# A two-layer graph network: POOL no longer drained at block ends, last iteration of the second loop written out, last two node units on places of their own

## The chip, the cores and the metric

One core of one Trainium2 chip runs the whole program. The metric is the device time of one execution in microseconds; the median of several runs counts. Engines are named as in the profile: PE (matmul), PEld (its weight load), DVE (vector), ACT (scalar), POOL (GpSimd) and SP (the sync engine, which here only issues DMAs). A trailing q (POOLq, SPq, PEldq) is the engine's sequencer.

## The reference, cut to what matters

6250 nodes of 128 features, 106250 edges sorted by receiver. Two layers, each with a residual and a layer norm around it:

```python
x = layernorm(x + L0(x, edge_attr_3, edge_weight, src, dst))        # loop 1
# L1, loop 2:
msg_in = concat(x[src], x[dst]); per type t: h = relu(msg_in @ W1[t] + b1[t]); m = h @ W2[t] + b2[t]
msgs = m * sigmoid(msg_in @ attn_w[t] + attn_b[t]) where edge_type == t
agg  = zeros.at[dst].add(msgs)
r = sigmoid(gi_r + gh_r); z = sigmoid(gi_z + gh_z); n = tanh(gi_n + r * gh_n)   # gi = agg@w_ih+b_ih, gh = x@w_hh+b_hh
y = layernorm((1-z)*n + z*x + x)*gamma + beta                        # what L1 returns
out = layernorm(x + y)
```

The inner layer norm takes (1-z)n + zx + x; the outer one is taken over the sum with x once more. So each node goes through: sums, gates, candidate, blend, transposition to rows, a first norm, gamma, x, beta, a second norm, store.

## The kernel before, in words

**Blocks.** The program is a row of blocks: `prepare` (tables, indices and the first gathers; its block is line 335), `edges0` (loop 1, line 717), `leftover0` (line 1172, work that is skipped when nothing is left), `edges1` (loop 2, line 1531), `leftover1` (line 1172 again). Within a block each engine runs its own list and they meet by semaphores; at a block's end every engine executes a DRAIN and then all meet at a barrier before the next block begins.

**Loops.** Both loops run over 104 steps of 1024 edges (8 tiles of 128), in 26 iterations of 4 steps (SLOTS), one for each of four gather buffers. `gather_loop` (line 605 in `gather_step`) makes POOL issue 8 indirect DMAs for each step; before it issues them it waits that the buffer was used (`used`). `prepare` already issues the gathers of steps 0 to 2 of loop 1, loop 1's block those of step 3 on. Loop 1 needs them in `messages` (line 659), loop 2 in `edge_rows` (line 1906).

**A step j of loop 2.** PE multiplies, for step j + 1, windows of the receivers' table (`receivers`, line 1754). DVE adds the gathered rows (`hid`, line 1906), builds the receivers' one-hot for step j + 2 (`rows_hot`, line 1865), adds step j - 1's sums to the accumulator (`adds`, lines 1887 and 1890, each 4 pairs), builds the one-hot of step j + 1 (`one_hot`, line 1873) and the scores (line 1922). ACT takes score and relu (lines 1651 and 1655) and issues the window loads of step j + 2 (`load_windows`, line 1535) and a key row of step j + 4 (`load_row`). PE then forms the step's sums (lines 1818 and 1824), for which `adds` waits.

**Node units.** In the same loop, 3 iterations behind, units of 256 nodes whose sums are complete go through the update, spread over the steps: PE `node_sums` (lines 1764, 1765), ACT `copy_sums` (1661), PE `node_gates` (1773, 1774), ACT `gates` (1666), PE `node_candidates` (1778, 1779), DVE `candidate` (1951, 1954), ACT tanh (1671), DVE `blend` (1959 to 1965), PE `node_rows` (1785), DVE `new_rows` (1970 and `moments`, 1928 to 1936), `residual` (1944 to 1984 and `moments`), `result` (1944), SP `store` (1611). SP loads x (`load_x_t` 1603, `load_x_row` 1607). All units share one set of buffers (`unit_area`) and two PSUM banks (`ps_v`).

**The tail.** Units 0 to 21 are finished within the loop; unit 22 is blended in the last step. After the loop come the last `adds(103)`, the rows of unit 22 and, one behind the other in the shared buffers, units 23 (256 nodes) and 24 (the last 128). There POOL takes the inverse square roots (`pow`, line 1642), between gathers none. The order on PE and DVE is written out:

```python
node_rows(g - 1, UN); node_sums(g, n, STEPS); node_gates(g, n); node_candidates(g, n)        # PE
node_sums(g2, n2, STEPS); node_rows(g, n); node_gates(g2, n2); node_candidates(g2, n2); node_rows(g2, n2)
adds(STEPS - 1, 1); new_rows(g - 1); candidate(g); residual(g - 1); blend(g); result(g - 1)   # DVE
new_rows(g); candidate(g2); residual(g); blend(g2); result(g); new_rows(g2); residual(g2); result(g2)
```

SP handles each unit in the order load x_t, store of the unit before, load x_row. `new_rows` waits until the store of the unit before has landed, since it writes the same `mid`. The last iteration does some work for steps 104 and 105, which do not exist: window loads in steps 102 and 103, a receivers' one-hot in both, `receivers` and `one_hot` in step 103.

## Time and profile before

| | us |
|---|---|
| median of 3 runs (2250.91 to 2253.52) | 2253.49 |
| profiled execution, its own time | 2254.85 |
| its span, first to last instruction | 2253.1 |
| busy: PE, DVE, ACT, POOL | 1810, 1477, 1347, 1609 |
| loop 1's gathers, first to last issue | 54.8 to 1112.1 |
| loop 2's gathers, first to last issue | 1149.3 to 2199.7 |

Times in the rows are microseconds from the span's start, unless marked ns. "Idle before <- X" is how long the engine stood still before an instruction and what ended it; "issue" means nothing that the profile shows. Busy shares are averages over stages with different limits, so the stages are read one by one: two long loops, the seams between blocks, and a tail of about 50 us after the last gather.

### The profile page before, as it was taken

The numbers are of one execution on the slowest core, as the hardware profiler recorded it, in microseconds if no ns is written. First come the engines' busy times: TensorE is split into PE (matmuls) and PEld (weight loads), VectorE is DVE, ScalarE is ACT, GpSimd is POOL, SyncE is SP. The second block draws the span as 40 slices with busy tenths as digits, with TensorE's granted clock in tenths as the row PEclk, the third lists the DMA queues.
The fourth block names the chain that finished last, engine by engine and source line by source line (L and its number), as shares of the span: only waits on it lengthen the run. The fifth ranks groups of instructions, "written<-read, shape, count | busy, mean of one in ns | idle before, by whom it ended". The sixth has DMA issues, their size and how long they took to land. (4 is left out here: it accounts for less than half of the span.)

```text
span 2253.1 us, 43663 instructions
## 1 busy us (share of the span) xinstructions
PE 1810.1 (80%) x10012; PEld 1436.0 (64%) x10012; DVE 1476.7 (66%) x3701; ACT 1347.0 (60%) x4416; POOL 1608.6 (71%) x1699
## 2 busy tenths in 40 slices
PE   7598999999999999999867876766667666676664
PEld 4276666666666766666646766666656666666663
DVE  4566555555655656556546777777777777777775
ACT  2587877777777777777634544544545545454451
POOL 2777777777777777777546777777777777777771
PEclk7599999999999999999979988887887888888886
DMA  6522323323233232333257855445454544544541
GB/s 205 153 54 56 79 74 82 80 72 87 75 82 80 73 85 75 81 80 82 67 168 210 225 118 123 109 118 115 111 122 108 120 115 110 123 109 117 117 110 32
DMA packets 222343, 236.65 MB, mean 105 GB/s; under 512 B 73015, under 2 KB 163295, under 8 KB 222157
## 3 DMA queue, kind: packets, MB, share of 16 engines
q0 software_dynamic: 53808, 112.80, 21.9%
q10 hardware_dynamic: 90012, 58.96, 10.4%
q1 hardware_dynamic: 78481, 64.43, 9.4%
q8 instruction: 14, 0.23, 0.0%
q14 instruction: 28, 0.23, 0.0%
HBM read 191.66 MB, written 44.35 MB: 105 GB/s over the span
## 5 line engine op out<-in xcount | busy, mean ns | idle before, releaser
L605 POOL DMA_INDIRECT gx<-node_d,idx x832 | 798.9, 960 | 265.8 <-issue 259.6
L605 POOL DMA_INDIRECT gp<-p_tab_d,idx x832 | 792.1, 952 | 261.5 <-issue 251.5
L677 ACT ACTIVATE msg<-ws,y 128x32 f32<-128x32 f32 x2496 | 552.8, 316 | 64.5 <-DVE ws L656 64.1
L908 PEld LDWEIGHTS ps_a<-hot,msg 128*128 128x128 f32 x3328 | 408.5, 197 | 194.4 <-issue 113.2
L1754 PE MATMUL ps_e<-win,hot_x 128*128 128x129 f32 x1680 | 300.2, 351 | 272.4 <-DVE hid L1906 249.5
L908 PE MATMUL ps_a<-hot,msg 128*128 128x128 f32 x3328 | 431.8, 285 | 61.5 <-DVE msg L665 40.2
L1754 PEld LDWEIGHTS ps_e<-win,hot_x 128*128 128x128 f32 x1680 | 275.8, 256 | 295.2 <-DVE hid L1906 266.0
L659 DVE TENSOR_TENSOR vy<-gx,y 128x768 f32<-128x768 f32 x104 | 99.6, 958 | 334.1 <-DMA gx<-node_d,idx 334.0
L1655 ACT ACTIVATE hid<-hid,score 128x128 f32<-128x128 f32 x832 | 278.7, 395 | 10.1
L1906 DVE TENSOR_TENSOR hid<-ps_e,gp 128x387 f32<-128x387 f32 (+1 forms) x312 | 142.0, 510 | 147.2 <-DMA gp<-p_tab_d,idx 140.0
L638 PE MATMUL ps_w<-w,h 128*128 128x256 f32 x832 | 221.5, 412 | 0.0
L1818 PEld LDWEIGHTS ps_g<-hot,hid 128*128 128x128 f32 x1664 | 212.9, 200 | 7.7 <-issue 1.1
L1818 PE MATMUL ps_g<-hot,hid 128*128 128x128 f32 x1664 | 212.6, 283 | 0.9 <-ACT hid L1655 0.7
L1651 ACT ACTIVATE score<-hid 128x3 f32<-128x3 f32 (+1 forms) x312 | 61.3, 196 | 245.2 <-DVE hid L1906 240.5
L638 PEld LDWEIGHTS ps_w<-w,h 128*128 128x128 f32 x832 | 158.2, 200 | 67.2 <-issue 48.0
L186 ACT ACTIVATE h<-ps_h,b 128x512 f32<-128x512 f32 x208 | 142.1, 683 | 95.4 <-PE ps_h L191 83.2
L1865 DVE TENSOR_TENSOR hot_x<-key_row,ps_s 128x1024 f32<-128x1024 bf16 x106 | 128.4, 1212 | 32.7 <-PE ps_s L1824 28.2
L1887 DVE TENSOR_TENSOR acc<-acc,ps_g 128x128 f32 x416 | 119.5, 287 | 13.5 <-issue 0.9
L1873 DVE TENSOR_TENSOR hot<-ps_s,key 128x1024 f32<-128x1024 f32 x105 | 127.6, 1215 | 0.0
L1005 DVE TENSOR_TENSOR hot<-ps_a,dloc 128x1024 f32<-128x1024 f32 x104 | 126.6, 1217 | 0.0
L904 PE MATMUL ps_h<-emb,w 16*128 16x512 f32 x202 | 113.2, 640 | 0.0
L191 PE MATMUL ps_h<-h,w 128*128 128x512 f32 x208 | 109.6, 609 | 3.7 <-ACT h L186 3.7
(221 smaller groups left out, 2213.7 us busy)
## 6 DMA issues: line engine op xcount, KB each, us to landing
win<-q_tab_d ACTq DMA_DIRECT2D x416, 64.5 KB
key_row<-key_row_d ACTq DMA_DIRECT2D x102, 256.0 KB, 3.6
gx<-node_d,idx POOLq DMA_INDIRECT x832
gp<-p_tab_d,idx POOLq DMA_INDIRECT x832
p_tab_d<-acc SPq DMA_DIRECT2D x23, 516.0 KB
q_tab_d<-unit_area SPq DMA_DIRECT2D x36, 258.0 KB, 3.3
q_tab_d<-acc SPq DMA_DIRECT2D x5, 774.0 KB, 5.5
emb<-emb_d SPq DMA_DIRECT2D x102, 32.0 KB
```

The costliest lines, as they stand in the source:

```text
L186: e.activation(mlp[f"h{layer}"][:], mlp["ps_h"][:], ACT.Silu, bias=w[f"b{layer - 1}"][:]).then_inc(ok, 1)
L605: e.indirect_dma_start(out=buf[:, h, t, :], out_offset=None, in_=table, in_offset=bass.IndirectOffsetOnAxis(ap=idx[:, h, t:t + 1], axis=0) ...
L638: last = e.matmul(ps_w[:, 2 * t:2 * t + 2, :], h2[:, t * P:(t + 1) * P], w["w2"][:], start=False, stop=t % 2 == 1)
L677: last = e.activation(self.cols[1][:, tile, c, :], self.ws[:, tile, :], ACT.Copy, scale=y[:, c:c + 1])
L908: last = e.matmul(ps_a[:, h, b, :], msgs[h].tile(t, b), hot[:, h, t, :], start=t == 0, stop=t == TPS - 1)
L1005: e.tensor_tensor(hot[:, h], spread(ps_a[:, h, IOTA, :], 1, TPS), spread(w["dloc"][:, bass.ds(j * TPS, TPS)], 2, P), ALU.is_equal)
L1655: last = e.activation(hid[:, h, t, 0:H], hid[:, h, t, 0:H], ACT.Relu, scale=score[:, h, t:t + 1])
L1754: last = e.matmul(ps_e[:, q, at:at + PW], hot_x[:, h, t, :], win[:, h, t // 2, :], start=True, stop=True)
L1818: e.matmul(ps_g[:, h, t // 2, :], hid[:, h, t, 0:H], hot[:, h, t, :], start=t % 2 == 0, stop=t % 2 == 1)
L1865: e.tensor_tensor(hot_x[:, h].rearrange("p t n -> p (t n)"), key_row[:, h, :], part.to_broadcast([P, TPS * P]), ALU.is_equal).then_inc(hx_ ...
L1873: e.tensor_tensor(hot[:, h], spread(iota[:, 0:P], 1, TPS), spread(k["key"][:, tiles], 2, P), ALU.is_equal).then_inc(hot_ok, 1)
L1906: e.tensor_tensor(hid[:, h, mine, :], ps_e[:, q, 0:n * PW].rearrange("p (t n) -> p t n", t=n), gp[:, u, mine, :], ALU.add).then_inc(pre_ok, 1)
```

## The change

Three things are done. (1) All blocks are made with `no_gpsimd_drain=True`, so POOL no longer executes a DRAIN at their ends; it still takes part in the barrier. The semaphores that only carry waits (`gate`, `gate_x`, `gate_v`) become one. (2) The last iteration of loop 2 leaves its loop on PE and DVE (on ACT it was already written out), and the work for steps 104 and 105 is gone from it. In step 103 DVE does `adds(102)` ahead of `edge_rows` and `blend(22)` ahead of the scores; PE does `node_sums` of unit 23 in the place of `receivers`. For that, the lower bound of the window of step 103 (and of none before it) rises from node 5888 to 6144; its edges begin at node 6203. (3) Units 23 and 24 get buffers and banks of their own: unit 23 keeps the usual places but for x_t, x_row and mid, which lie in gather buffer 1; unit 24 has all in gather buffer 0 and the banks of `ps_e`, with counters of its own; unit 22's rows go to a third bank. Their loads wait for steps 100 and 101 to have used the buffers, and stand ahead of the stores. The written-out orders of SP, POOL, ACT, PE and DVE behind the loop are interleaved.

```diff
+BOUND = (NT - 1) * P
+            gate=m.sem("gate"),
...
-        with nc.Block() as block:
+        with nc.Block(no_gpsimd_drain=True) as block:
...
-                own.then(e.scalar_tensor_tensor(startf[:], past, float(LAST), startf[:], ALU.min, ALU.max))
+                own.then(e.scalar_tensor_tensor(startf[:], past, float(BOUND), startf[:], ALU.min, ALU.max))
...
+        usual = dict(places(unit_area, UN), sums=ps_u[:, 0], gates=ps_u[:, 1], rows=ps_u[:, 1], at=0, own_f=own_f, own_n=own_n,
+                     var_ok=var_ok, root_ok=root_ok)
+        spare = [gp[:, u].rearrange("p t f -> p (t f)") for u in range(2)]
+        before_rest = dict(usual, rows=ps_e[:, 2])
+        first_rest = dict(usual, at=2, **{name: spare[1][:, c * UN:(c + 1) * UN] for c, name in enumerate(("x_t",))},
+                          **{name: spare[1][:, c * UN:(c + 1) * UN].rearrange("p (b f) -> p b f", f=H)
+                             for c, name in ((1, "x_row"), (2, "mid"))})
+        last_rest = dict(places(spare[0], P), sums=ps_e[:, 0], gates=ps_e[:, 1], rows=ps_e[:, 1], at=4, own_f=end_f, own_n=end_n,
+                         var_ok=end_var, root_ok=end_root)
...
+                for (g, n), z, u in zip(REST, (first_rest, last_rest), (1, 0)):
+                    e.wait_ge(used, SLOTS + STEPS - SLOTS + u + 1)
+                    e.wait_ge(xt_ld, 16 * g)
+                    load_x_t(g, n, z)
+                    e.wait_ge(xr_ld, 16 * g)
+                    load_x_row(g, n, z)
+                store(UNITS - 1, UN, usual)
+                for (g, n), z in zip(REST, (first_rest, last_rest)):
+                    store(g, n, z)
...
-                    e.wait_ge(win_in[h], 16 * PPS * (STEPS // 2 + 1))
-                    e.wait_ge(row_in[h], 16 * (STEPS // 2 + 1))
+                    e.wait_ge(win_in[h], 16 * PPS * (STEPS // 2))
+                    e.wait_ge(row_in[h], 16 * (STEPS // 2))
...
-                for g in range(UNITS - 1, UNITS + 2):
-                    for c in range(2):
-                        e.wait_ge(var_ok, g * 2 + (c + 1))
-                        e.tensor_tensor(rstd[:], rstd[:], minus_half[:], ALU.pow).then_inc(root_ok, 1)
+                def root(g, n, c, z):
+                    mine = rstd[:, z["at"]:z["at"] + n // P]
+                    e.wait_ge(z["var_ok"], own_count(g, z) * 2 + (c + 1))
+                    e.tensor_tensor(mine, mine, minus_half[:, 0:n // P], ALU.pow).then_inc(z["root_ok"], 1)
+
+                (g, n), (g2, n2) = REST
+                for c in range(2):
+                    root(g - 1, UN, c, before_rest)
+                for c in range(2):
+                    root(g, n, c, first_rest)
+                    root(g2, n2, c, last_rest)
...
-                        e.wait_ge(e_mm, i * (NQ * SLOTS) + (NQ * u + NQ))
+                        if not last or u < SLOTS - 2:
+                            e.wait_ge(e_mm, i * (NQ * SLOTS) + (NQ * u + NQ))
-                        load_windows(e, regs, j + 2, h)
+                        if not last or u < SLOTS - 2:
+                            load_windows(e, regs, j + 2, h)
...
-                        if not last or u + SLOTS < SLOTS + 2:
+                        if not last:
...
-                for g, n in REST:
+                (g, n), (g2, n2) = REST
+                copy_sums(g, n, first_rest)
+                gates(g, n, first_rest)
+                copy_sums(g2, n2, last_rest)
+                candidate(g, n, first_rest)
+                gates(g2, n2, last_rest)
+                candidate(g2, n2, last_rest)
...
-                    e.wait_ge(cand_ok, g + 1)
+                    if z is not last_rest:
+                        e.wait_ge(cand_ok, g + 1)
...
-                    e.wait_ge(mid_ok, g + 1)
+                    if z is usual:
+                        e.wait_ge(mid_ok, g + 1)
                     for c in range(2):
...
-                def steps(i, unit, before, table=False):
+                def steps(i, unit, before, table=False, final=False):
                     for u in range(SLOTS):
                         h, j = u % 2, i * SLOTS + u
-                        e.wait_ge(hx_ok, j + 2)
-                        e.wait_ge(win_in[1 - h], i * (16 * PPS * SLOTS // 2) + 16 * PPS * (u // 2 + 1 + h))
-                        for q in range(NQ):
-                            e.wait_ge(pre_ok, i * (NQ * SLOTS) + (NQ * u + q + 1))
-                            receivers(1 - h, q)
+                        if not final or u < SLOTS - 1:
+                            e.wait_ge(hx_ok, j + 2)
+                            e.wait_ge(win_in[1 - h], i * (16 * PPS * SLOTS // 2) + 16 * PPS * (u // 2 + 1 + h))
+                            for q in range(NQ):
+                                e.wait_ge(pre_ok, i * (NQ * SLOTS) + (NQ * u + q + 1))
+                                receivers(1 - h, q)
+                        else:
+                            node_sums(*REST[0], STEPS - 1, first_rest)
...
-                with e.Fori(LAG + 1, LOOPS) as i:
+                with e.Fori(LAG + 1, LOOPS - 1) as i:
                     steps(i, True, True)
+                steps(LOOPS - 1, True, True, final=True)
...
-                node_rows(g - 1, UN)
-                node_sums(g, n, STEPS)
-                node_gates(g, n)
-                node_candidates(g, n)
-                node_sums(g2, n2, STEPS)
-                node_rows(g, n)
-                node_gates(g2, n2)
-                node_candidates(g2, n2)
-                node_rows(g2, n2)
+                node_rows(g - 1, UN, before_rest)
+                node_gates(g, n, first_rest)
+                node_candidates(g, n, first_rest)
+                node_sums(g2, n2, STEPS, last_rest)
+                node_gates(g2, n2, last_rest)
+                node_candidates(g2, n2, last_rest)
+                node_rows(g, n, first_rest)
+                node_rows(g2, n2, last_rest)
...
-                    if before:
-                        e.wait_ge(sum_mm, j)
-                    rows_hot(h, i * (16 * SLOTS // 2) + 16 * (u // 2 + 2))
+                    if not final or u < SLOTS - 2:
+                        if before:
+                            e.wait_ge(sum_mm, j)
...
                         e.wait_ge(zero_ok, 5)
-                    if before:
+                    if final and u == SLOTS - 1:
+                        blend(i - LAG, UN)
+                    elif before:
                         adds(j - 1, 1 - h)
-                    one_hot(bass.ds(j * TPS + TPS, TPS), 1 - h)
+                    if not final or u < SLOTS - 1:
+                        one_hot(bass.ds(j * TPS + TPS, TPS), 1 - h)
...
+                def new_rows(g, n, z=usual):
-                    e.wait_ge(y_st, g * 16 + 16)
-                    e.tensor_copy(mid[:, 0:n // P, :], ps_u[:, 1, 0:n].rearrange("p (b f) -> p b f", f=H))\
+                    if z is usual or z is before_rest:
+                        e.wait_ge(y_st, g * 16 + 16)
...
+                def steps(i, first, unit, before, last=False):
                     for u in range(SLOTS):
-                        edge_rows(i, u, not first or u > 0, first and u == 1)
+                        if last and u == SLOTS - 1:
+                            adds(STEPS - 2, 0)
+                        edge_rows(i, u, not first or u > 0, first and u == 1, last)
...
-                        if unit and u == 3:
+                        if unit and u == 3 and not last:
...
-                with e.Fori(LAG + 1, LOOPS) as i:
+                with e.Fori(LAG + 1, LOOPS - 1) as i:
                     steps(i, False, True, True)
+                steps(LOOPS - 1, False, True, True, last=True)
                 adds(STEPS - 1, 1)
...
-                new_rows(g - 1, UN)
-                candidate(g, n)
-                residual(g - 1, UN, True)
-                blend(g, n)
-                result(g - 1, UN, True)
-                new_rows(g, n)
-                candidate(g2, n2)
-                residual(g, n, True)
-                blend(g2, n2)
-                result(g, n, True)
-                new_rows(g2, n2)
-                residual(g2, n2, True)
-                result(g2, n2, True)
+                new_rows(g - 1, UN, before_rest)
+                candidate(g, n, first_rest)
+                residual(g - 1, UN, before_rest, True)
+                candidate(g2, n2, last_rest)
+                blend(g, n, first_rest)
+                result(g - 1, UN, before_rest, True)
+                blend(g2, n2, last_rest)
+                new_rows(g, n, first_rest)
+                new_rows(g2, n2, last_rest)
+                residual(g, n, first_rest, True)
+                residual(g2, n2, last_rest, True)
+                result(g, n, first_rest, True)
+                result(g2, n2, last_rest, True)
```

## Rows read from the trace of the kernel before

**Rows 1.** Waits of DVE over the whole span: engine, line <- awaited: us, times, longest
```profile
DVE vy L659 <- DMA gx<-node_d,idx: 334.0, 94, 5.6
DVE hid L1906 <- DMA gp<-p_tab_d,idx: 140.0, 90, 3.1
```

**Rows 2.** Line L605, POOL's gathers: ns min/median/max, and what its idle time ended on
```profile
L605 POOL DMA_INDIRECT gx<-node_d,idx x832: 942/947/2987, 54.8 to 1112.1; - x167
...
  issue: 511.0, 1649
  POOLq L335: 6.2, 1
...
  DVEq L1912: 4.0, 13
```

**Rows 3.** Line L335, end of the block of prepare: duration ns, start us
```profile
L335 POOLq DRAIN  x1: 23297/23297/23297, 71.7 to 71.7; - x1
...
L335 SPq DRAIN  x1: 7/7/7, 85.4 to 85.4; - x1
```

**Rows 4.** Timeline of POOL, the first gather of loop 1's block: start us, us
```profile
95.99 0.94 POOL L605 DMA_INDIRECT gx<-node_d,idx  x1 [6.24 <-POOLq L335]
```

**Rows 5.** Lines L717 and L1172, ends of the blocks of loop 1 and of the leftovers
```profile
L717 POOLq DRAIN  x1: 17367/17367/17367, 1100.5 to 1100.5; - x1
...
L717 SPq DRAIN  x1: 7/7/7, 1145.3 to 1145.3; - x1
...
L1172 POOLq DRAIN  x2: 125/129/133, 1146.5 to 2252.6; - x2
```

**Rows 6.** Timeline of the tail, DVE: last step, last adds, unit 23's candidate
```profile
2203.76 1.36 DVE L1906 TENSOR_TENSOR hid<-ps_e,gp 128x387 f32<-128x387 f32 x3 [2.89 <-DMA gp<-p_tab_d,idx]
...
2212.05 0.29 DVE L1887 TENSOR_TENSOR acc<-acc,ps_g 128x128 f32 x1 [0.48 <-issue]
...
2222.03 0.48 DVE L1951 SCALAR_TENSOR_TENSOR unit_area<-ps_v,b_hh,unit_area 128x256 f32<-128x256 f32 x1 [5.98 <-ACT unit_area L1666]
```

**Rows 7.** Timeline of the tail, PE: start us, us, operation, idle before it
```profile
2204.38 3.63 PE L1754 MATMUL ps_e<-win,hot_x 128*128 128x129 f32 x16 [3.97 <-DVE hid L1906]
2207.80 2.06 PE L1818 MATMUL ps_g<-hot,hid 128*128 128x128 f32 x16
2210.07 0.71 PE L1824 MATMUL ps_s<-hot_n,sc 128*128 128x128 f32 x4 [0.21 <-DVE sc L1922]
...
2214.51 3.44 PE L1764 MATMUL ps_v<-acc,w 128*128 128x256 f32 x8 [2.45 <-DVE acc L1887]
```

**Rows 8.** Timeline of the tail, ACT: relu of the last step, copy of unit 23's sums
```profile
2206.83 0.70 ACT L1655 ACTIVATE hid<-hid,score 128x128 f32<-128x128 f32 x2
...
2218.63 0.38 ACT L1661 ACTIVATE unit_area<-ps_v 128x256 f32<-128x256 f32 x1 [11.10 <-PE ps_v L1765]
```

**Rows 9.** Stretches, busy us of each engine, granted clock: PE after idling
```profile
2205.00:2208.00 3.00, 3.00 (x15) 3.00 (x15) 2.80 (x10) 2.46 (x9) 0.00 (x0) 0.50 0.00 0
```

**Rows 10.** Timeline of PE: sums of an earlier unit
```profile
1294.29 1.89 PE L1764 MATMUL ps_v<-acc,w 128*128 128x256 f32 x8
```

**Rows 11.** Stretch from DVE's last add to the last store's start
```profile
2214.50:2246.75 32.25, 12.35 (x47) 9.39 (x47) 16.11 (x60) 3.04 (x8) 4.30 (x6) 0.61 0.06 17
```

**Rows 12.** Waits of DVE from 2214.5 to 2247 us
```profile
DVE unit_area L1970 <- DMA out<-unit_area: 4.0, 2, 2.0
DVE unit_area L1951 <- PE ps_v L1779: 2.5, 1, 2.5
DVE unit_area L1944 <- POOL rstd_v L1642: 1.6, 2, 0.8
```

**Rows 13.** Line L1531, end of the block of loop 2
```profile
L1531 POOLq DRAIN  x1: 6031/6031/6031, 2245.6 to 2245.6; - x1
...
L1531 SPq DRAIN  x1: 7/7/7, 2248.6 to 2248.6; - x1
```

**Rows 14.** Timeline of PE in loop 2's other written-out iteration
```profile
1303.76 3.53 PE L1754 MATMUL ps_e<-win,hot_x 128*128 128x129 f32 x16 [3.41 <-issue]
```

198 lines of the change are left out of this document (103 added, 95 removed).

## The prediction

> **What bounds the kernel now.** I read DVE's waits first, then POOL's gathers, then the ends of the blocks, last the tail instruction by instruction. DVE waits for gathered rows in 94 of 104 steps of loop 1 and 90 of 104 of loop 2 [rows 1]. POOL, which issues them, hardly waits: a gather takes 0.95 us, the gap behind it 0.31 (511.0 us over 1649 gaps), and the waits for a used buffer in loop 2 come to 4.0 us in all [rows 2]. So both loops last as long as 832 gathers take to issue, and what counts is when POOL's rows of gathers begin and what follows the last of them.
>
> At the end of `prepare` POOL's DRAIN lasts from 71.7 to 95.0, while SP, the last of the others, is at the barrier at 85.4 [rows 3]. POOL's next gather comes at 95.99, after 6.24 us in which POOL had nothing to issue [rows 4]. This is the one hole in the gathers of loop 1 [rows 2]. At the end of loop 1 the DRAIN (1100.5 to 1117.9) is long over when SP arrives at 1145.3, and at the leftover blocks, with no work before it, it takes 0.13 us [rows 5].
>
> The tail: the last gathers land at 2203.7 [rows 6], the last store starts at 2246.75 [rows 11], and DVE is busy for only 16.1 of the last 32.25 us of that [rows 11]. At the end POOL's DRAIN holds the barrier until 2251.6, while SP is there at 2248.6 [rows 13].
>
> **The change, part by part.**
>
> *No DRAIN after `prepare`.* POOLq passes its barrier at once (it had handed out its gathers by 71.7), so the block ends at 85.4, 9.6 us sooner. POOL is then still issuing the gathers of steps 0 to 2, and those of step 3 join on: the gap of 6.24 becomes 0.31. All later gathers of loop 1 come 5.9 us sooner. The buffers allow it, as DVE too begins 9.6 us sooner, and nothing else in loop 1 sets POOL's pace; loop 1's end, its seam and loop 2 follow. **5.9 us**; bounds 0 and 9.6.
>
> *No DRAIN at the other ends.* After loop 1: 0, covered by the 27 us until SP comes [rows 5]. The two leftover blocks: at most 0.13 each, **0.2** together. After loop 2: the barrier comes at SP's 2248.6 in place of 2251.6, **3.0**; bounds 0 and 3.0. One shared semaphore for `gate`: 0, nobody waits on it.
>
> *Work for steps that do not exist.* ACT's window loads of steps 102 and 103, and DVE's one-hot in step 102, stand beside the wait for gathers (DVE idles 2.89 us before step 103 [rows 6]): 0 here, and nothing if the cover went, since the work goes away. The higher bound of step 103's window lies below its edges: 0.
>
> *Step 103 on DVE.* `adds(102)` takes 2.45 us by the later `adds` (2212.05 to PE's start at 2214.51 [rows 6, 7]) and goes into the idle 2.89. Some 0.1 us of it may stick out; I take 0. Then `hid`, `blend(22)`, scores: these are done at about 2207, when ACT begins its last relu [rows 8], before PE wants them. They were what held PE's score sums before (0.21 us of waiting for DVE at 2210.07 [rows 7]).
>
> *Step 103 on PE.* `receivers` goes (3.6 us after 3.97 idle [rows 7]) and the sums of unit 23 come in its place. They wait for `adds(102)`, so they begin at 2204.0, and queued behind them on PE are the sums of step 103, for which `adds(103)` waits. After such an idle time PE runs at half its clock (0.50 from 2205 to 2208, that is 1.2 GHz [rows 9]), and unit 23's sums took 4.1 us at that level (2214.51 to ACT's copy at 2218.63 [rows 7, 8]) against 1.89 for four fifths of them at full clock [rows 10]. So PE is free at 2208.1, 0.3 later than the 2207.80 of before; ACT's relu is done by then, at 2207.5 [rows 8]. With 2.06 and some 0.6 less overlap [rows 7], `adds(103)` begins at 2210.6 in place of 2212.05: **1.5 us**. If PE were at full clock there it would be ready at 2206.4, relu would decide, and the gain would be about 3.
> The Trainium skill, TensorE: Matmul & The Clock Gate, Part 1, says that the half rate is the state after idling and that activity lifts it; it speaks against putting new matmuls first after a wait. By that rule, and by [rows 9], the sum has 1.5 here; without it the sum would have 3.
>
> *Units 23 and 24.* From the first operation behind `adds(103)` to the last store DVE needs 32.25 us. Of these 5.98 are the wait for unit 23's sums, gates and candidate [rows 6], and 4.0 the waits until a store has landed, 2.5 the wait for unit 24's gates (behind its load of x_t), 1.6 two waits for POOL's `pow` [rows 12].
> The 5.98 goes: sums and their copy are done at 2208.5; from the copy to DVE's 2222.03 it took 3.4 us [rows 6, 8], now 3.0 from 2210.6 on with 0.4 for unit 22's transposes in front, so ready at 2214.0. DVE begins `new_rows(22)` at 2213.0 and needs 1.55 for it (2222.03 less 5.98 less 2214.50), and comes at 2214.6. The 4.0 goes, with `mid` buffers of their own. The 2.5 goes: the loads of x now wait only for gather buffers that steps 100 and 101 have used, and stand ahead of the stores on SP; and unit 24's products follow on PE from 2214.0: at half clock about 2.0 (half of 4.1), 0.3 and 3.0 (as for unit 23), 2219.3, while DVE has unit 23's candidate and unit 22's residual before it (12 of its 60 operations of that stretch [rows 11], so about a fifth of the 18.4 us that are left) and comes at 2218.3; at full clock it waits for nothing. PE has been busy since 2204 without a pause, so I take full clock and 0, with 1.0 as the bound. Of the two `pow` waits the first is covered by unit 23's work and 0.2 of the second stays: 1.4 gone. DVE's own work is unchanged. **13.9**; bounds 11 and 14.
>
> Sum: 5.9 + 0.2 + 3.0 + 1.5 + 13.9 = **24.5 us**. The profiled execution took 2254.85 us (span 2253.1), so 2230.4; it lay 1.4 above the median of the runs, from which the same sum gives 2229.0. I put down 2229.5.
>
> **The rivals.**
> *A. The hole of 6.24 us does not count.* If something else set loop 1's pace in its first iterations, the earlier gathers would only wait longer in their buffers. Against it: 94 waits for gathers, and POOL without any other hole [rows 1, 2]. 2229.5 + 5.9 = 2235.4. Chance 0.09.
> *B. PE stays at half clock in the tail.* The step's sums then take about 3.6 instead of 2.06 (16 products, [rows 7]) and gates and candidates some 2.5 more: 4 us, 2233.5. For it: most of the old tail ran so (0.61 in the mean [rows 11]). Against it: PE now has work without pause. Chance 0.08.
> *C. Written-out code is late.* Nearest rows: PE stood 3.41 us for no shown reason in the other iteration that is written out [rows 14], DVE 0.48 on leaving its loop [rows 6]. Only in step 103 would it hurt: 2232.9. The Trainium skill, Runtime: NRT & Kernel Launch, Instruction fetch mechanics, says that fetching runs ahead in straight code and breaks on taken branches, which speaks against this rival. Chance 0.05.
> *D. The change does not free the barrier.* If POOL's arrival still waits for its own work to retire, 5.9, 3.0 and 0.2 are lost: 2238.6. Chance 0.04.
> *E. More than the sum.* The whole 9.6 counts and unit 23's sums run at full clock: 3.7 + 1.5 more, 2224.3. Chance 0.08.
> *F. Slower.* Without the DRAINs the queue of gathers is never emptied, and issuing one takes longer, as it does where it is crowded (2987 ns at worst against 947 [rows 2]). Some 1640 gathers stand behind `prepare`; at 20 ns more for each they cost 33 us, 2262; from 15 ns on the gain is gone. Against it: POOL issues over 800 in a row at 947 ns without a DRAIN. Chance 0.02.
>
> **How the numbers follow.** The forecast has the remaining 0.64. The range, 2224 to 2237, takes in A, B, C, most of E and the bounds of the parts; D and F lie outside. A measurement of this kernel tells about 0.2% (4.5 us) from no change. All cases but F are faster by more: 0.97; F is split, 0.01 and 0.02.
>
> **What would show it.** Line by line in the profile after: no hole above 1 us in POOL's gathers near 90; the last gather of loop 1 about 5.9 sooner, the last of loop 2 about 6.0 sooner (2193.7); from there to the last store about 32 us in place of 47; unit 23's sums taking 4.1 us in front of the last step's; DVE waiting for nothing above 1 us behind the last `adds`; SP's arrival, not POOL's, ending the block. A last gather of loop 2 at 2199 shows A; waits of DVE for PE in the tail show B or C; POOL as the last at the barriers shows D; a mean gather above 0.97 us shows F.

## The result, and the profile after

The changed kernel took 2219.73 us in the median of four runs (2217.45 to 2223.25), beside 2252.20 us for the kernel before (four runs, 2250.24 to 2253.52): ratio 0.986, 95% interval 0.9845 to 0.9876. It is 32.5 us faster where 24.5 were forecast, and it lies below the forecast range. Three later series gave 0.9890 (0.9872 to 0.9909), 0.9894 (0.9864 to 0.9923) and 0.9886 (0.9867 to 0.9905), that is 26.4, 23.9 and 26.1 us; the forecast's 24.5 us, from 2254.0 to 2229.5, are a ratio of 0.9891. So there are two questions: which parts gave more than their term, and what the 8 us between the series are. (In one series, that of the runs e5 to e8, every kernel had a median of 3012 to 3029 us, the one before too.)

The profiled execution after was the fastest of its four (2217.45 us, span 2215.7), the one before above all of its own (2254.85). These are the gathers after, in the view of [rows 2]; the last two lines answer to [rows 1]:

```profile
L607 POOL DMA_INDIRECT gx<-node_d,idx x832: 940/944/2474, 51.0 to 1098.5; - x167
L607 POOL DMA_INDIRECT gp<-p_tab_d,idx x832: 938/944/1209, 1136.4 to 2182.9; - x167
...
  issue: 509.0, 1643
  DMA idx<-p_idx_d: 6.6, 6
  DVEq L1960: 4.3, 14
  POOLq L337: 0.3, 1
...
  DVE vy L661: 337.5, 96
  DVE hid L1953: 133.4, 90
```

The hole behind `prepare` (6.2 us in [rows 2, 4]) is an ordinary gap of 0.3 now. The loops are bound as before: some 90 waits for gathers in each. But the first gather is already 3.8 us sooner (51.0 against 54.8), ahead of every place that the forecast priced. The end of the block of `prepare`, and POOL's gathers across it, answer to [rows 3, 4]:

```profile
L337 SPq EVENT_SEMAPHORE  x2: 17/17/17, 80.4 to 80.6; - x2
L337 POOLq EVENT_SEMAPHORE  x2: 17/17/17, 80.4 to 80.5; - x2
...
L337 SPq DRAIN  x1: 7/7/7, 80.3 to 80.3; - x1
```
```profile
79.43 0.94 POOL L607 DMA_INDIRECT gx<-node_d,idx  x1 [0.30 <-issue]
80.68 0.94 POOL L607 DMA_INDIRECT gx<-node_d,idx  x1 [0.30 <-POOLq L337]
```

SP and POOL leave the barrier together, with SP's arrival at 80.3 as the last; POOL has a gather on either side of it.

The timeline of the tail after, PE and DVE, answers to [rows 6, 7]:

```profile
2183.22 0.29 DVE L1934 TENSOR_TENSOR acc<-acc,ps_g 128x128 f32 x1
...
2185.57 2.70 PE L1807 MATMUL ps_v<-acc,w 128*128 128x256 f32 x8 [2.62 <-DVE acc L1934]
2187.14 1.36 DVE L1953 TENSOR_TENSOR hid<-ps_e,gp 128x387 f32<-128x387 f32 x3 [1.67 <-DMA gp<-p_tab_d,idx]
...
2189.11 2.56 PE L1865 MATMUL ps_g<-hot,hid 128*128 128x128 f32 x16
...
2191.50 0.61 PE L1871 MATMUL ps_s<-hot_n,sc 128*128 128x128 f32 x4
...
2192.24 0.29 DVE L1934 TENSOR_TENSOR acc<-acc,ps_g 128x128 f32 x1 [1.78 <-PE ps_s L1871]
...
2194.34 0.42 DVE L2027 COPY unit_area<-ps_e 128x256 f32<-128x256 f32 x1
...
2195.80 0.48 DVE L2006 SCALAR_TENSOR_TENSOR unit_area<-ps_v,b_hh,unit_area 128x256 f32<-128x256 f32 x1
...
2211.84 0.35 DVE L1998 TENSOR_SCALAR gp<-gp,mv_v,rstd_v 128x128 f32<-128x128 f32 x1 [0.19 <-POOL rstd_v L1672]
```

Unit 23's sums (L1807) run ahead of `hid(103)`; unit 23's candidate (L2006), which waited 5.98 us in [rows 6], has no wait shown; the one wait for another engine behind the last `adds` is 0.19 us for POOL's `pow`. And the end of the block of loop 2, against [rows 13]:

```profile
L1554 SPq EVENT_SEMAPHORE  x2: 17/17/17, 2214.2 to 2214.3; - x2
L1554 POOLq EVENT_SEMAPHORE  x2: 17/17/17, 2214.2 to 2214.3; - x2
```

With the further runs of both kernels there are three normal profiles of the kernel before (the first, e1, e16) and four of the changed one (the first, e2, e9, e14). The table cuts their spans at the same events, in us; hid(103), adds(103) and new_rows(22) stand for the start of DVE's first operation of that name:

| stretch | before | after | mean | forecast |
|---|---|---|---|---|
| start to first gather | 54.8, 54.6, 49.7 | 51.0, 52.2, 50.9, 49.7 | -2.1 | 0 |
| POOL's gap at the end of prepare | 6.2, 7.3, 4.8 | 0.3, 0.3, 0.3, 0.3 | -5.8 | -5.9 |
| the rest, first to last gather | 2138.6, 2139.3, 2135.4 | 2131.6, 2132.0, 2133.5, 2141.5 | -3.2 | -0.2 |
| last gather to hid(103) | 4.1, 4.1, 4.0 | 4.3, 4.6, 4.4, 4.8 | +0.4 | 0 |
| hid(103) to adds(103) | 8.3, 8.3, 8.3 | 5.1, 5.1, 5.1, 6.3 | -2.9 | -1.5 |
| adds(103) to new_rows(22) | 2.5, 2.5, 2.5 | 2.1, 2.1, 2.1, 2.1 | -0.4 | 0 |
| new_rows(22) to DVE's end | 32.2, 32.1, 31.8 | 17.9, 17.9, 17.9, 17.9 | -14.2 | -13.9 |
| DVE's end to the span's end | 6.4, 6.4, 6.4 | 3.5, 3.6, 3.6, 3.6 | -2.9 | -3.0 |

The mean spans differ by 30.9 us (2250.2 and 2219.3). In six rows the profiles of the two kernels do not overlap, and these six sum to 25.7 us (means before rounding). In the first and third they do; their 5.3 us need another explanation.

### The profile page after: what moved, and what is told of

Its sections match the earlier page's. It is cut to its first block and busy times, and to the rows that moved or that the text cites. A ratio compares the mean times of both kernels' runs of the same rounds, so it can differ in the third digit from the quotient of the medians.

```text
span 2215.7 us, 43530 instructions
## 1 busy us (share of the span) xinstructions
PE 1788.7 (81%) x9996; PEld 1423.4 (64%) x9996; DVE 1471.5 (66%) x3696; ACT 1342.9 (61%) x4416; POOL 1601.9 (72%) x1699
```

## The experiments

**Both kernels once more** (e1, e2: no edit) and **the drains alone**, without the rest of the change (e3) and the other way round (e4). Edit of e3, at L335, L717, L1172 and L1531 of the kernel before (e4: the reverse in the changed kernel):

```diff
-        with nc.Block() as block:
+        with nc.Block(no_gpsimd_drain=True) as block:
```

> The kernel before once more, unchanged. Between the two traces 26.6 us of the gain lie where parts of the change act (prepare's end 5.9, tail 17.8, program end 2.9), and 11.4 us do not: the first gather begins 3.8 us sooner, and POOL's gathers of both loops take together 7.6 us less (mean of one in loop 1 960 against 956 ns). Theory V, variation: the profiled execution of before was its slowest run (2254.9 us), so a new profile has a first gather between 51 and 55 us and gathers of 956 to 960 ns with no edit at all; time 2252, ratio 1.000. Rival I, the gathers' issue is truly quicker after the change: the new profile shows 54.8 us and 960 ns again, within 1 ns.

> The changed kernel once more. Time 2219.7, ratio 0.986. Theory V: the first gather falls anywhere between 51 and 55 us, the mean gather of loop 1 anywhere between 956 and 960 ns, as in the kernel before. Rival I: 51.0 us and 956 ns again, below every profile of before.

> The kernel before with POOL's DRAIN left out at the ends of the four blocks and nothing else. Theory P, the drains are worth what stands at their two places (hole 5.9 + program end 3.1 + leftover blocks 0.2): 9.2 us less, 2243.0, ratio 0.9959. Rival I: the missing DRAINs also make the gathers' issue quicker, another 5.9 us or so (the measured 32.5 less the 26.6 at the parts' places): 2237, ratio 0.9933. Rival H, the hole does not reach the end because the gathers wait for it later anyway: only 3.3 us, 2249, ratio 0.9985.

> The changed kernel with POOL's DRAIN put back at the ends of all four blocks; the tail of loop 2 and the shared gate semaphore stay. Theory P: 9.2 us more than the changed kernel, 2228.9, ratio to before 0.9896. Rival I: 15 us more, 2235, ratio 0.9922. Rival H: 3.3 us more, 2223, ratio 0.987. Where the ratio stands at 0.9896 but the kernel before without drains gains less than 9.2 us, the two parts of the change help each other.

Measured, the kernel before at 2249.54: e1 2250.21 (0.9997, 0.9982 to 1.0012; runs from 2239 to 2256), e2 2223.18 (0.9890), e3 2240.33 (0.9956, 0.9940 to 0.9971), e4 2233.04 (0.9925, 0.9908 to 0.9942). The drains are worth 9.2 us in the kernel before (the interval gives 6.5 to 13.5) and 9.9 in the changed one (some 5 to either side), against 9.1 in the sum (5.9 + 0.2 + 3.0): theory P. Rivals I and H fall by e3, whose interval takes in neither 0.9933 nor 0.9985. That the two halves of the change help or hinder each other is not seen, within those 5 us. E4 is also the other half timed by itself: with all DRAINs in place the rest of the change saves 16.5 us (0.9908 to 0.9942, 13 to 21 us), where the sum had 15.4. The mean gather of loop 1 was 960 and 967 ns in the two profiles of the kernel before, and 956 and 958 in those of the changed one, so it moves by 7 ns with no edit. The first gather had not moved with the kernel, though: 54.6 in e1, 54.7 in e3, 52.2 in e2, 50.8 in e4.

**Loads put back, sums put back, gates apart, small edits alone** (e5 to e8). In e5 ScalarE loads windows and key rows for missing steps again; in e6 unit 23's sums go behind the loop; in e7 each block has gate semaphores of its own; e8 is the kernel before with the one gate and with BOUND.

```diff
@@ e5, the changed kernel, ScalarE
-                        if not last or u < SLOTS - 2:
-                            e.wait_ge(e_mm, i * (NQ * SLOTS) + (NQ * u + NQ))
+                        e.wait_ge(e_mm, i * (NQ * SLOTS) + (NQ * u + NQ))
...
-                        if not last or u < SLOTS - 2:
-                            load_windows(e, regs, j + 2, h)
+                        load_windows(e, regs, j + 2, h)
...
-                        if not last:
+                        if not last or u < 2:
                             e.wait_ge(hx_ok, j + 3)
                             load_row(e, j + 4, h)
@@ e6, the changed kernel, TensorE
-                        else:
-                            node_sums(*REST[0], STEPS - 1, first_rest)
...
                 node_rows(g - 1, UN, before_rest)
+                node_sums(g, n, STEPS - 1, first_rest)
                 node_gates(g, n, first_rest)
@@ e7, the changed kernel
-        clear, gate = m.sem("clear"), k["gate"]
+        clear, gate = m.sem("clear"), m.sem("gate_p")
...
-        gate = gate_x = k["gate"]
+        gate, gate_x = m.sem("gate0"), m.sem("gate_x0")
...
-        gate = gate_v = k["gate"]
+        gate, gate_v = m.sem("gate_1"), m.sem("gate_v1")
```

> The changed kernel with ScalarE's loads of windows and key rows for the steps that do not exist put back in the last iteration (the rest of the change stays; SP waits for them at its end). Of the tail 20.4 us went where 18.5 were forecast, and 1.7 of the surplus lie between hid(103) and the first adds(103) (8.3 us in before, 5.1 in the changed kernel, forecast 6.8). Theory L: that surplus comes from ScalarE, whose loads stood ahead of the root that result(21), adds(102) and so unit 23's sums wait for: adds(103) comes 1.5 to 2 us later again, time 1.7 us more than the changed kernel, ratio 0.9897 beside its 0.989. Rival N: the surplus comes from the work taken off VectorE and TensorE in the last steps: no more than 0.3 us, adds(103) stays at 5.1 us after hid(103).

> The changed kernel with the node sums of unit 23 moved from the last step of the loop to behind it, ahead of that unit's gates; nothing else. Theory W, by the trace of the changed kernel: the eight matmuls and two more (2.7 and 1.06 us) then begin at 2192.3 instead of 2185.6, candidate(23) waits on VectorE for them, their copy, gates and candidates: about 4 us more, time 2227, ratio 0.9908; VectorE shows one wait of 4 us at that candidate. Rival C: at full clock the sums cost half of that and moments(22) cover some: 2 us more. Rival D: VectorE's waits are hidden by the order of the units' work: nothing.

> The changed kernel with gate semaphores of their own in each block again (five as in the kernel before), nothing else. In three profiles of the kernel before or of it without drains, TensorE stayed at half clock from 30 to 56 us and the first gather began at 54.6 to 54.8 us; in three of the changed kernel, with drains or without, it had full clock from 32 to 43 us and the first gather began at 50.8 to 52.2. Theory V: this is chance of the execution: the first gather falls at either, time 2223, as the changed kernel. Rival G: the shared semaphore is what moved it: first gather at 54.7 and 3 us more. In both the mean gather stays within 1 ns per instruction of 956.

> The kernel before with the two small edits of the change alone: one gate semaphore for all blocks, and the bound of the window starts one node tile later (BOUND in place of LAST). Theory V: nothing, 2249.5, ratio 1.000, first gather at 54.7 or 51. Rival G: first gather at 51 to 52, 3 us less, ratio 0.9987. If ratio and first gather stay as in the kernel before, neither edit explains the earlier gather.

Measured beside 3028.53 us for the kernel before: e5 3012.6 (0.9946), e6 3013.5 (0.9944), e7 3013.7 (0.9938), each about 0.003 wide to either side, and e8 3025.1 (0.9994, 0.9968 to 1.0020). E8's edits do nothing that shows; its first gather came at 53.1. For the others the series says little, so three ran again beside the changed kernel:

> The changed kernel beside the three that follow, on the same chip. In the last series the kernel before took 3028 us instead of 2250 in all its runs (stalls of 6 to 8 us that stop TensorE at 'issue' in every step of both loops), so that its ratios say little of a tail of 30 us; this one is to give them again. Where the kernel before takes 2250, this takes 2220 to 2223, ratio 0.986 to 0.989, and the time from the last gather to the end is 33 us. Where it takes 3028 again, only the tail and prepare can be compared.

> As the earlier run of the changed kernel with ScalarE's loads of windows and key rows for missing steps put back. Theory L: adds(103) comes 1.5 to 2 us later after hid(103) than in the changed kernel (5.1 us), time 1.7 us more than the changed kernel of this series. Rival N: no more than 0.3 us.

> As the earlier run of the changed kernel with unit 23's node sums behind the loop. Theory W: VectorE waits some 4 us at candidate(23), time 4 us more than the changed kernel of this series. Rival C: 2 us more. Rival D: nothing. In the slow series the time from the last gather to the end was 43.1 us here against 41.6 in the kernel with separate gates, which would speak for C.

> As the earlier run of the changed kernel with gate semaphores of its own in each block. So far TensorE had full clock from about 30 to 40 us in five of five profiles of kernels with the shared semaphore and the new tail, and half clock in the five others (three of the kernel before, one with these separate gates, one of the kernel before with the shared one). Theory V, chance: either. Rival G, a property of the program as built: half clock from 30 to 44 us and a first gather at 54 us here again, and 3 us more than the changed kernel of this series.

Measured beside 2252.09: e9 2228.15 (0.9894), e10 2226.63 (0.9879), e11 2228.94 (0.9897), e12 2228.01 (0.9885), intervals of about 0.003 to either side. E9 was expected at 2220 to 2223 and came 5 us above; from the last gather to the end it took 33.0 us, as expected. E12's first gather came at 49.4, with PE back at full clock at 30 us, so rival G falls: gates of its own do not bring the late gather. The times can't part the other three; the tails can. First the loads. Unit 23's sums and the last `adds` in e10, then `hid(102)` and `adds(102)` in e10, then `hid(102)` in e9:

```profile
2198.04 1.97 PE L1805 MATMUL ps_v<-acc,w 128*128 128x256 f32 x8 [2.48 <-DVE acc L1932]
...
2203.07 0.29 DVE L1932 TENSOR_TENSOR acc<-acc,ps_g 128x128 f32 x1 [1.78 <-PE ps_s L1869]
```
```profile
2186.97 1.36 DVE L1951 TENSOR_TENSOR hid<-ps_e,gp 128x387 f32<-128x387 f32 x3
...
2195.69 0.29 DVE L1932 TENSOR_TENSOR acc<-acc,ps_g 128x128 f32 x1 [0.77 <-PE ps_s L1869]
```
```profile
2177.16 1.36 DVE L1953 TENSOR_TENSOR hid<-ps_e,gp 128x387 f32<-128x387 f32 x3 [0.35 <-DMA gp<-p_tab_d,idx]
```

With the loads unit 23's sums begin 0.07 us behind `hid(103)` (2197.97) instead of 0.2 to 2.7 ahead, so theory L is right about the start. Its path, ScalarE's root, is not what the rows show. The root is ready 1.6 to 1.9 us before DVE takes it in all eleven other profiles with the new tail, and 0.1 before in e10, where `adds(102)` then waits 0.77 us more for the score sums of step 102. Those are late in e4, e13 and e17 as well, which have no such loads: in these four profiles PE worked at half clock through the whole of step 102's `receivers` (3.78 us). What goes with the loads lies earlier: step 102 begins sooner without them. `hid(102)` starts 6.1 to 6.7 us ahead of the last gather in the five profiles that load key rows for steps 104 and 105 (three of the kernel before, e3, and e10 with 2186.97 against 2193.31), and 7.4 to 7.6 ahead in the eleven that do not (e9: 2177.16 against 2184.61). Of the loads put back in e10 only these key rows, issued in steps 100 and 101, stand ahead of `hid(102)`; the window loads of steps 102 and 103 come behind it. No run put either back alone, so that the key rows are the cause is argued from this order, not shown.

But `adds(103)` stays at 5.1 us behind `hid(103)`, as rival N has it: the loads move the start and not the end. What moves the end is PE's clock, as the sums of the last step show in e12 and in e11 beside the 2.56 us of the changed kernel (above):

```profile
2199.70 3.75 PE L1865 MATMUL ps_g<-hot,hid 128*128 128x128 f32 x16 [0.62 <-ACT hid L1692]
...
2204.33 0.29 DVE L1934 TENSOR_TENSOR acc<-acc,ps_g 128x128 f32 x1 [3.27 <-PE ps_s L1871]
```
```profile
2192.34 3.76 PE L1863 MATMUL ps_g<-hot,hid 128*128 128x128 f32 x16 [6.69 <-ACT hid L1692]
...
2196.91 0.29 DVE L1933 TENSOR_TENSOR acc<-acc,ps_g 128x128 f32 x1 [3.21 <-PE ps_s L1869]
```

Where those 16 products take 2.2 to 2.6 us (eight profiles of the changed kernel and its variants with the sums in place) `adds(103)` begins 5.1 us after `hid(103)`; where they take 3.75 (e12, e14, e15) it is 6.3 to 6.6. The early start alone does not help: it was the longest of all in e15 (2.7 us). In e11 PE has nothing ahead of them, idles 6.69 us, works at half clock and reaches 6.5 as well. The one case with both, sums that begin 0.07 us behind `hid(103)` and half clock over all of them (3.75 us), is e7: there `adds(103)` comes 7.4 us behind `hid(103)`, later than in any other profile of the new tail. The granted clock of the stretches says the same, in the first profile after and in e12 (us, then busy us of PE, PEld, DVE, ACT and POOL, the clock, the share of DMA, GB/s):

```profile
2188.00:2190.00 2.00, 2.00 (x7) 1.26 (x6) 1.74 (x6) 1.97 (x8) 0.00 (x0) 0.50 0.34 98
2190.00:2192.00 2.00, 2.00 (x19) 2.00 (x19) 0.46 (x3) 1.13 (x5) 0.00 (x0) 0.98 0.16 41
```
```profile
2199.00:2201.00 2.00, 1.38 (x7) 1.34 (x7) 1.74 (x7) 1.93 (x8) 0.00 (x0) 0.50 0.37 107
2201.00:2203.00 2.00, 2.00 (x11) 2.00 (x11) 0.05 (x1) 0.75 (x3) 0.00 (x0) 0.50 0.14 33
```

E11 also shows what the sums' new place is worth: from the last gather to the end 36.8 us against 33.0 in e9, 3.8 more, with a wait of 2.03 us at unit 23's candidate and 1.4 more ahead of `adds(103)`. That is theory W's 4 us by the trace. Part of it is PE's clock in the last step: against e12 and e14, which ran that step at half clock with the sums in place (34.7 and 34.6), e11 is 2.1 us longer, rival C's 2. The timed runs (2228.94 against 2228.15) can't tell these apart.

**Fillers for the clock, the drain after prepare alone, both kernels again** (e13 to e16; e14 and e16 without an edit).

> The changed kernel with 44 matmuls more in prepare (weights times weights, into a PSUM bank that is overwritten next), put where TensorE stands idle from 18.7 to about 25 us; the result stays the reference's. They tell whether the 3.4 us by which the first gather came sooner in the changed kernel's profiles (54.7 us before, 51.0, 52.2 and 50.9 after) are TensorE's clock. Theory K: TensorE is then at full clock from the 16-row matmuls at 25 us on (1.12 us for two instead of 2.04), the first gather begins at 47 to 50 us, and the time is 1 to 4 us under the changed kernel of this series, ratio 0.987. Rival R: the loads and stores of prepare set the first gather and the clock only goes along: first gather at 50 to 52 as before, no gain; where the 44 products delay the 16-row matmuls, up to 1 us lost.

> The changed kernel beside the others of this series: 2220 to 2228, ratio 0.986 to 0.990. Theory V, that the clock's rise in prepare is chance of the execution: the first gather falls anywhere between 50 and 55 us.

> The changed kernel with POOL's DRAIN put back at the end of prepare alone. Theory P: a hole of 4 to 7 us in POOL's gathers near 90 us, 6.5 us more than the changed kernel of this series, the end of the program as without drains (3.5 us after VectorE's last instruction). Rival H: the hole is there and costs nothing. With all four drains back the cost was 9.9 us (2233.0 against 2223.2).

> The kernel before beside the others of this series: 2250, ratio 1.000. Theory V: the first gather falls anywhere between 50 and 55 us, so that one profile in some shows TensorE at full clock before 40 us. Rival G', a property of the program as built: half clock from 25 to 56 us and first gather at 54.7 for the fourth time.

```diff
@@ e13, the changed kernel, TensorE, widen(0)
                     if s == 0:
+                        for n in range(44):
+                            e.matmul(ps_b[0][:, 0:P], w_up[:], w_up[:], start=True, stop=True)
                         e.wait_ge(row_clear, 1)
@@ e15, the changed kernel, prepare
-        with nc.Block(no_gpsimd_drain=True) as block:
+        with nc.Block() as block:
```

PE's timeline in `prepare`, a stretch of e16 (the kernel before) and the same of e15 (the changed kernel with one drain):

```profile
28.12 3.36 PE L558 MATMUL ps_w<-w_up,gx 128*128 128x128 f32 x14
31.41 1.12 PE L568 MATMUL ps_b<-acc,of_row 16*128 16x512 f32 x2
```
```profile
29.34 3.35 PE L560 MATMUL ps_w<-w_up,gx 128*128 128x128 f32 x14
32.62 2.07 PE L570 MATMUL ps_b<-acc,of_row 16*128 16x512 f32 x2
```

Here the roles are turned round: the kernel before gets full clock at 31 us (1.12 for two products) and its first gather at 49.7; the changed kernel with one drain stays at half clock (2.07) and has its first gather at 55.3. So the early gather belongs to the execution and not to the change: theory V, and rival G' falls. Timed, beside 2250.76: e14 2224.65 (0.9886), e15 2229.17 (0.9907, 0.9887 to 0.9926), e16 2246.24 (0.9985, 0.9971 to 0.9998). The last is the unchanged kernel: two groups of runs of the same kernel in one series can stand 4.5 us apart. E15 costs 4.5 us more than e14, with an interval of 5 to 6 to either side, so by itself it does not rule out that the hole is free (rival H); its hole was 6.6 us, and its program ends 3.6 us behind DVE, as without DRAINs.

E13 took 2220.14 (0.9865, 0.9846 to 0.9885), 4.5 us less than e14 with intervals that overlap. PE was at full clock until 42 us, but the 44 products took 10 us and pushed the 16-row products to 28.4; the first gather came at 50.7, no sooner than chance gives. Hence a shorter filler (e17), and one in the tail as well (e18):

```diff
@@ e17 and e18, the changed kernel, TensorE, widen(0)
+                        for n in range(22):
+                            e.matmul(ps_b[0][:, 0:P], w_up[:], w_up[:], start=True, stop=True)
@@ e18 alone, last step of the loop
                         else:
+                            for n in range(8):
+                                e.matmul(ps_u[:, 1, 0:P], k["ident"][:], k["ident"][:], start=True, stop=True)
                             node_sums(*REST[0], STEPS - 1, first_rest)
```

> The changed kernel with 22 matmuls in the idle time of prepare instead of 44. The 44 took 10 us (each passes twice, 113 ns a pass), three more than the gap: the 16-row matmuls began at 28.4 instead of 23.3 to 26.6, and the first gather at 50.7, inside the spread of the changed kernel (49.7 to 55.3). Theory K: 22 end at 23.5, before the data are there, and TensorE keeps full clock: two 16-row matmuls in 1.12 us from 24 to 26 us on, first gather at 47 to 49, ratio 0.985. Rival R: the first gather stays at 49.5 to 51 although the clock is full, because the stores of the node table set it; then nothing beyond the kernel with 44 (0.9865). Rival C: TensorE falls to half clock again in the gap of 1 to 3 us that is left, and the first gather is at 50 or 55 by chance.

> The same, and 8 such matmuls ahead of unit 23's node sums, into a PSUM half that nothing holds any more, where TensorE waits 2.6 us for adds(102). In the tail adds(103) began 5.1 us after hid(103) where TensorE had full clock when the last step's sums ran (five profiles), and 6.3 to 6.6 where it had half (three, this kernel's unchanged form among them): chance too. Theory K: 5.1 us for certain, about 0.6 us less in the mean; together with the 22 in prepare ratio 0.985. Rival C: the 8 delay the node sums, or the clock falls in spite of them: 5.1 to 6.6 as before.

Measured beside 2248.37: e17 2217.83 (0.9866, 0.9848 to 0.9885), e18 2220.65 (0.9876, 0.9859 to 0.9894). Rival C: in e17 PE kept full clock over the gap of 1.3 us, for one pair of products, and lost it all the same:

```profile
18.59 5.08 PE L567 MATMUL ps_h<-w_up 128*128 128x128 f32 x44
24.97 1.09 PE L572 MATMUL ps_h<-acc,of_row 16*128 16x512 f32 x2 [1.30 <-DMA acc<-length_d]
25.90 1.46 PE L572 MATMUL ps_x<-acc,of_row 16*128 16x512 f32 x2
27.29 3.36 PE L560 MATMUL ps_w<-w_up,gx 128*128 128x128 f32 x14
30.58 2.07 PE L572 MATMUL ps_b<-acc,of_row 16*128 16x512 f32 x2
```

Its first gather came at 53.1. In e18, with the same fillers and a gap of 2.7 us, the clock fell too and was back at 33 us; the first gather came at 51.4. In e18 the 8 products kept PE at full clock for the sums behind them (1.97 us) and for the last step's (2.55), and `adds(103)` at 5.1, which is also the usual case without them. None of the three can be told from the changed kernel, whose ratios run from 0.9860 to 0.9894; a version that is better for certain was not found.

## Why the prediction was right or wrong

*No DRAIN after prepare: right.* 5.9 forecast; the gap is 5.8 us shorter in the mean. Putting the drain back there alone cost 4.5 us, with an interval that does not part this from nothing; rival A (the hole does not count) falls by e3, which it would have near 3.3 us instead of 9.2. Rival D (the barrier is not freed) falls with the rows of L337.

*The other ends: right.* 3.0 forecast, 2.9 measured, and 2.4 in e3 by its whole tail (50.9 us against 53.3). The 0.2 for the leftover blocks can't be seen: from loop 1's last gather to loop 2's first it took 37.0 to 37.3 before and 36.9 to 37.8 after.

*Units 23 and 24: right in mechanism and size.* 13.9 forecast, 14.2 measured, 17.85 to 17.87 us in all four profiles of the changed kernel. The waits of [rows 12] are gone, and of the `pow` waits 0.2 is left, as put down. The choice between the bounds 11 and 14 was full clock behind the last step. It held where it counted: from 6 us behind `hid(103)` at the latest until 13 to 16 us behind it the granted clock was full in all four, and unit 24's candidate products are done 11 to 12 us behind it. From there to the end PE was at half clock, and DVE waited for none of it.

*Step 103 on PE: the step that failed.* The term was 1.5; it measured 2.9 in the mean and 3.2 in three of four. The prediction had unit 23's sums begin 0.2 us *after* `hid(103)` and hold PE for 4.1 us, with the last step's sums queued behind until 2208.1 and `adds(103)` at 2210.6. They began 1.6 to 2.3 us *ahead* of `hid(103)` in those four profiles. The rows show where these 1.8 to 2.5 us come from:
- Some 0.7 are in the prediction's own numbers: DVE is idle from 2200.87 (2203.76 less 2.89), so an `adds(102)` of 2.45 us is over at 2203.3, not at 2204.0.
- 0.7 to 0.9 are `hid(102)`, which stands 7.4 to 7.6 us ahead of the last gather, against 6.7 in the profile before. It does so wherever the loads of key rows for steps 104 and 105 are gone. Work for missing steps was put at 0.
- 0.2 to 0.7 are `hid(103)` itself, which comes later behind the last gather (below), and the last 0.2 DVE's own work between `hid(102)` and the sums.

The price of the sums was about right: with their last two products they took 3.6, 4.1 and 3.6 us in three of the four profiles (the first, e2, e14), mostly at half clock, and 2.4 in e9 at full clock. But begun that early they are out of the way when the last step's own products can start, 2.0 us behind `hid(103)`, at either clock. Then ACT's last relu decides (3.75 us behind `hid(103)` in every profile), the case for which the prediction had written "about 3" and not taken it. Full clock alone would have done the same: in e10 the sums begin 0.07 behind, take 2.4 us, and `adds(103)` is at 5.1. Only both together, late and at half clock, cost as much as was forecast, and more; that was e7 (7.4 us where the forecast has 6.8). What cost time in the changed kernel is half clock in the last step's own sums (3.75 instead of 2.56): 1.2 us, in e14, one of its four profiles.
The rule cited beside the term (the Trainium skill, TensorE: Matmul & The Clock Gate, Part 1: half rate after idling, lifted by activity) agrees with three of these four: PE idled 2.6 to 2.9 us ahead of unit 23's sums and was at half clock within 1.1 us of their start; in e9, after 2.61 us, it kept full clock. So the clock was not what the term had wrong, and taking the rule out would have reached 3 for a reason that the rows do not bear out. Whether the new matmuls keep the clock up for the last step is not shown: without them (e11, and e6) PE idled 6.69 and 5.15 us and ran that step at half clock, but with them it did so in three of eleven profiles too (e12, e14, e15). The other half of the rule does not hold everywhere: in `prepare` activity without a pause did not lift the clock (below).

*Small terms.* 0.4 us were lost between the last gather and `hid(103)`, in the mean, in four profiles of four; the loads of x now stand there, but the runs did not single them out (e10 has 4.7, e13 and e17 3.8 and 3.9 with the same loads). 0.4 came from the last `adds`, whose two short pauses "issue" shrank.

*The parts together* give 25.7 us where the sum had 24.5: 1.2 too little, nearly all of it in the failed term. That alone would have left the time inside the range. The signs put down say the same: in the first profile after, the last gather to the last store's start took 29.3 us where about 32 were forecast, while the last gathers of the loops came 13.6 and 16.8 us sooner, not 5.9 and 6.0. The other 5 us of the profiles and the 8 us between the first series and the third are scatter: the first gather falls from 49 to 55 us in either kernel and goes with PE's clock in `prepare`, and the gathers' own time (third row of the table) spread over 2128.0 to 2143.5 us in the sixteen profiles outside the series of e5 to e8, before and after alike (e3, a kernel before, 2132.8; e12, a changed one, 2143.5). Why the gathers' own time spreads so is open. The second thing that failed is therefore the range, and it is what put the first measurement outside: its lower end counted bounds of the parts (E: 3.7 us from the whole 9.6 and 1.5 from the clock) and no scatter of the medians, of which the two sets of runs shown told too little. That the three later ratios lie within 0.0005 of the forecast's is partly luck, as their intervals are 0.002 to 0.003 to either side. Rival E had the right side; of its two parts the whole 9.6 did not come (5.8), and full clock over unit 23's sums came in one of four profiles. B's half clock came true for one step and not for the tail, C's late code did not show, and F's longer gathers did not either (956 to 964 ns after, 959 to 967 before).

## What to carry to other kernels

Price a barrier's drain by the wait it causes in the queue that bounds the kernel, and at the places where it is the last to arrive: here two of the ends were worth 5.8 and 2.9 us and the others nothing that shows, and the timed runs have 9.2 and 9.9 for all of them. When matmuls are moved into a gap, ask for the moment at which their input is ready under the *new* order on every engine, and work it out from the rows of the waiting engine: a start that is 2 us early can make their price vanish. Loads that are taken away count too; here the gathered rows of two later steps came sooner without them. Before giving a range, learn how far two sets of runs of one kernel lie apart; here that was 4.5 us in one series, more than three of the five terms.

## What the runs showed of the hardware that was not expected

TensorE's granted clock in `prepare` differs from execution to execution of the same program. After idling from 18.7 to about 25 us it is at half clock (1.2 GHz), and from there it worked without a pause at half clock until 56 us in the first profile of the kernel before, while in e16, the same program, it was at full clock from 31 to 42 us. In the seventeen profiles without fillers in `prepare` (those of e5 to e8 included) the granted clock rose at 30 to 34 us, at 39 to 40, at 45, or not before 76 us (five: the first of the kernel before, e1, e3, e7 and e15). The first gather goes with it: 49.4 to 52.2 us where the clock rose by 40, 53.1 where it rose at 45, 53.6 to 55.3 where it did not. No run forced the one to see the other follow; e13, which kept the clock up, also delayed the products. Work without a pause is thus no guarantee of full clock, and neither are 5 us of fillers ahead of a gap of 1.3 us (e17).

A product of 128x128 f32 by 128x128 f32 counts as two of 113 ns each at full clock: the 44 fillers of e13 are 88 instructions and 9.99 us.

Loads that nobody used seem to hold up gathered rows. In the five profiles with the key rows of 256 KB each for steps 104 and 105, issued in steps 100 and 101, `hid(102)` began 0.7 to 1.5 us later against the last gather than in the eleven without. In e10 `hid(101)`, which begins 4.3 us behind such a load, waited 2.95 us for its gathered rows. This goes by the order of time; no run put these loads back alone.

In the series of e5 to e8 all kernels took a third longer, on the same chip as e1 to e4 before and e9 to e12 behind it. The gathers there, of e8, beside the [rows 2] of before:

```profile
L607 POOL DMA_INDIRECT gx<-node_d,idx x832 | 806.1, 969 | 667.2 <-DVEq L1096 329.2 <-issue 249.0 <-DMA idx<-in_src 85.1
```

A gather takes hardly longer (969 ns against 960), nor does an operation of DVE or ACT; a product of loop 1's sums does (320 ns against 285, at a mean granted clock of 0.78 against 0.89). What grew most is the waiting of each engine for the others (POOL for DVE's queue 329 us in loop 1, where the first profile of the kernel before has none). From 600 to 622 us of e8, a stretch of loop 1, DVE and ACT stand still twice for 6 to 8 us. The first time they go on at 603.5, though the products that they read are on record as ended at 597.3 and 598.2, and PE's last one ahead of them at 601.6; the profile puts the end of these waits down to no engine of the core. The cause is open; no run tried it.
